# One product for two units: a windowed-attention pipeline's output projection, from float32 per unit to three float32r passes per pair

## The chip, the cores and the metric

The kernel runs on one core of a Trainium2 chip. The metric is device time in microseconds (us) of that core for one whole execution, as the median of several runs. The kernel before takes 2122.96 us (three runs, 2122.40 to 2123.63).

## The reference, cut to what matters

The program is a chain of layers over x of 8 x 512 tokens with 128 features. The change touches one kind of layer, used twice (`_L1_ffn_ref`, each time with two inner layers):

```python
def _layer(x, wqkv, qs, ksc, wo, lg, lb, w1, b1, w2, b2):
    h = shift_token(x)
    q, k, v = jnp.split(h @ wqkv, 3, axis=-1)          # 8 heads of 64: INNER = 512
    q, k = rotary_xpos(l2norm(q) * qs, l2norm(k) * ksc)
    o = local_attention(q, k, v)                        # windows of 64
    x = x + o @ wo                                      # 512 -> 128: the product of this case
    h = layer_norm(shift_token(x)) ; h = h @ w1 + b1
    a, g = jnp.split(h, 2, axis=-1)
    return x + (a * gelu(g)) @ w2 + b2
x = x + 0.5 * _L1_ffn_ref(layer_norm(x), ...)           # first of two uses
x = x + _L1_attn_ref(layer_norm(x), ...)
x = x + 0.5 * _L1_ffn_ref(layer_norm(x), ...)           # second
```

## The kernel before, in words

The program runs phases one after the other: two mixture-of-experts phases with a state-space phase between them, a setup of weights (`gated_setup_phase`), then `macaron_phase`, a short global phase, and `macaron_phase` again. Only the setup and the two macaron phases are touched.

A macaron phase treats 16 items (8 blocks of 512 tokens, for each of 2 inner layers), and each item is 4 units of 128 tokens. All engines run a software pipeline written out by hand: `item(i)` has one loop body for each t in 0 to 3, and that body is called **slot t** here. In a slot, the engines work on different units: with n the unit of the slot, TensorE makes the scores of n (`sims`), turns q and k of n+1 (`turn_qk`), makes attention times v of n-1 (`values`), projects q, k, v of n+3 (`project`), turns the probabilities of n (`turn_probs`, once for each of two halves r = 1 and r = 0), and makes the output product of n-1 (`output`). The parts of the gated feed-forward of an earlier item are spread over the slots: `up(.., 0, 2)` in slot 0, `centre` and `variance` in slot 1, `down` and three `up` in slot 2, two `up` in slot 3. In time order one item of the trace is slot 2, 3, 0, 1.

Each engine takes its instructions in the written order. Engines meet at semaphores. Those that matter here:

- `sims` (lines 1551, 1555, 1562) writes PSUM banks 2 and 3, which hold the turned probabilities of the unit before until ScalarE has copied them (`keep_turned`, line 1744). So `sims` waits for `pt_kept` of both halves.
- `turn_qk` (line 1533) writes banks 0 and 1, which VectorE reads in `rotate` (line 1830, two instructions a unit). It waits for `rotated`.
- `turn_probs` (line 1573) waits for `shared`: GpSimd multiplies the probabilities by the reciprocal sums (line 2058).
- `values` writes PSUM bank 4 (`O`), `keep_out` on VectorE (line 1881) copies it to `ot`, `output` (line 1600) multiplies by `wo` into the first 128 columns of O, and `add_out` (line 1889) adds that to the residual `u`.
- `f_take` on GpSimd (lines 1979, 1980), in slot 0, waits until all units of its item are added to `u`, and stands in GpSimd's queue ahead of `add(n + 3)` (line 2038) and so of the next slot's `share` (line 2058).

VectorE's order in a slot is `maxima` (1864), `keep_qt` (1857), `norms` (1841), `reciprocals` (1873), feed-forward pieces, `keep_out` (1881), `clip` (1849), `rotate` (1830), `add_out` (1889), `maxima` of the next unit (1864).

A float32 matmul stands in the trace as two rows, one for each of its passes over the array; a float32r matmul as one. `mm3` (lines 54 to 56) is a product in three float32r passes: high by high, low by high, high by low. Another phase, mixture of experts, has float32r matmuls of fewer columns, which the prediction reads:

```python
pe.matmul(bank[:, :2 * P], gh[:, q % 2, k, :], at(2 * P), start=k == 0, stop=False)      # line 384, 256 columns
mm = pe.matmul(bank[:, :P], gl[:, q % 2, k, :], at(P), start=False, stop=k == HC - 1)    # line 385, 128 columns
```

## Time and profile before

| | |
|---|---|
| median of 3 runs | 2122.96 us |
| profiled execution: its time, its span | 2117.76 us, 2115.9 us |
| TensorE matmul busy / weight loads busy | 1819.0 us (86%) / 1388.3 us (66%) |
| VectorE, ScalarE, GpSimd busy | 1571.3 us (74%), 1398.0 us (66%), 1284.5 us (61%) |
| mean granted TensorE clock | 0.937 of full speed |
| macaron phases, roughly | 660 to 1270 us and 1480 to 2100 us |

Busy time is the sum of an engine's rows. Matmul rows overlap, since each includes the way through the array, so a busy TensorE says only that its queue did not run dry; the pace is read from the starts of rows. PE is TensorE, PEld its weight loads, DVE VectorE, ACT ScalarE, POOL GpSimd.

### The profile page before, as it was taken

What the parts mean: (1) busy time and instruction counts of PE and PEld (TensorE: products, weight loads), DVE (VectorE), ACT (ScalarE), POOL (GpSimd) and SP (SyncE); (2) the same over time, 40 slices, a digit from 0 to 9 for tenths busy, and PEclk for the clock granted to TensorE, in tenths of its full rate; (3) what the DMA queues carried; (4) which work ended last, traced back from release to release, by engine and by line L of the source; (5) the groups of instructions that cost most, each with busy time, mean ns of one, the idle gap of its engine ahead of it and who ended that gap; (6) DMA issues with size and microseconds to landing.
All of it is one profiled execution on the core that took longest, in us unless ns stands there. A gap on an engine that the chain in (4) does not pass through costs nothing. (4 is left out here: it accounts for less than half of the span.)

```text
span 2115.9 us, 51807 instructions
## 1 busy us (share of the span) xinstructions
PE 1819.0 (86%) x16844; PEld 1388.3 (66%) x16845; DVE 1571.3 (74%) x2828; ACT 1398.0 (66%) x3956; POOL 1284.5 (61%) x1099
## 2 busy tenths in 40 slices
PE   4499776289955999999999997766999999999996
PEld 3488623278833777777777774334777777777773
DVE  6788767778855888788788883335888787888882
ACT  5555441345544888888878874555878888888783
POOL 3674300666415888878788872005888788787870
PEclk9999888589967999999999998788999999999998
DMA  6332310133151111111110110000110111111101
GB/s 210 86 91 57 84 54 1 56 97 87 39 149 44 27 29 22 25 24 27 24 28 21 22 29 1 4 0 18 27 29 20 27 24 27 24 26 22 25 22 40
DMA packets 87308, 88.26 MB, mean 42 GB/s; under 512 B 13978, under 2 KB 65863, under 8 KB 87016
## 3 DMA queue, kind: packets, MB, share of 16 engines
q1 hardware_dynamic: 77288, 68.09, 12.9%
q0 software_dynamic: 8704, 17.85, 2.5%
q8 instruction: 88, 1.44, 0.3%
q14 instruction: 76, 0.62, 0.1%
q10 hardware_dynamic: 1152, 0.25, 0.1%
HBM read 35.60 MB, written 22.22 MB: 27 GB/s over the span
## 5 line engine op out<-in xcount | busy, mean ns | idle before, releaser
L2058 POOL TENSOR_TENSOR mac_probs<-mac_probs,mac_prec 128x512 f32<-128x512 f32 x256 | 265.0, 1041 | 194.3 <-DVE mac_prec L1873 193.8
L1734 ACT ACTIVATE mac_probs<-banks,mac_nmax 128x128 f32<-128x128 f32 x1024 | 358.7, 385 | 0.0
L1830 DVE TENSOR_TENSOR route_pool<-banks,tables 128x1024 f32<-128x1024 f32 x256 | 300.6, 1214 | 33.7 <-ACT route_pool L1694 28.3
L2038 POOL TENSOR_TENSOR route_pool<-route_pool 128x1024 f32<-128x1024 f32 x128 | 303.3, 2369 | 35.7 <-issue 13.1
L1864 DVE TENSOR_REDUCE mac_nmax<-banks 128x4 f32<-128x512 f32 x256 | 164.8, 685 | 125.0 <-PE banks L1562 125.0
L2049 POOL TENSOR_TENSOR mac_qkn<-route_pool,mac_rc 128x1024 f32<-128x1024 f32 x128 | 243.6, 1903 | 16.4 <-issue 7.3
L876 POOL DMA_INDIRECT x_sorted<-route_pool,route_index x128 | 125.7, 982 | 185.8 <-DVE route_index L680 102.8
L1734 ACT ACTIVATION_READ_ACCUMULATOR mac_probs<-banks,mac_nmax 128x1 f32 x1024 | 231.9, 226 | 0.0
L884 POOL DMA_INDIRECT y_tokens<-moe_bench,moe_goal x144 | 140.7, 977 | 118.1 <-DVE moe_bench L827 77.9
L54 PE MATMUL banks<-wqkv_h,mac_hh 128*128 128x512 f32 x384 | 179.5, 467 | 27.0 <-POOL mac_hl L2013 22.1
L1744 ACT ACTIVATE mac_pts<-banks 128x512 f32<-128x512 f32 x256 | 147.2, 596 | 43.1 <-PE banks L1573 40.4
L1724 ACT ACTIVATE mac_kt<-banks 128x512 f32<-128x512 f32 x128 | 76.5, 597 | 139.6 <-PE banks L1533 139.3
L1694 ACT ACTIVATE route_pool<-banks 128x1024 f32<-128x1024 f32 x128 | 129.3, 1010 | 56.9 <-PE banks L56 56.8
L1573 PEld LDWEIGHTS banks<-ident,mac_probs 128*128 128x128 f32 x1024 | 118.9, 140 | 67.3 <-POOL mac_probs L2058 42.0
L1573 PE MATMUL banks<-ident,mac_probs 128*128 128x128 f32 x1024 | 150.1, 277 | 14.1 <-POOL mac_probs L2058 13.7
L56 PE MATMUL banks<-wqkv_l,mac_hh 128*128 128x512 f32 x384 | 155.0, 404 | 0.0
L384 PE MATMUL banks<-w,moe_gh 128*128 x576 | 152.1, 341 | 3.0 <-DVE moe_gl L817 2.8
L1841 DVE TENSOR_REDUCE mac_ss<-route_pool 128x16 f32<-128x1024 f32 x128 | 154.5, 1207 | 0.0
L555 ACT ACTIVATE moe_gh<-banks 128x512 fp32r<-128x512 f32 x144 | 86.1, 598 | 103.6 <-PE banks L373 102.9
L55 PE MATMUL banks<-wqkv_h,mac_hl 128*128 128x512 f32 x384 | 154.1, 401 | 0.0
L1533 PE MATMUL banks<-ident,mac_qkn 128*128 128x128 f32 x1024 | 141.6, 282 | 7.2 <-DVE route_pool L1830 7.2
L1600 PE MATMUL banks<-mac_ot,wo 128*128 128x128 f32 x1024 | 137.0, 277 | 5.0 <-DVE mac_ot L1881 5.0
(321 smaller groups left out, 5015.3 us busy)
## 6 DMA issues: line engine op xcount, KB each, us to landing
mac_v_even<-mac_v SPq DMA_DIRECT2D x224, 128.0 KB, 2.2
moe_xs<-x_sorted SPq DMA_DIRECT2D x144, 72.0 KB
route_pool<-y_tokens SPq DMA_DIRECT2D x16, 512.0 KB, 7.2
y_tokens<-moe_bench,moe_goal POOLq DMA_INDIRECT x144, 2.3
moe_bench<-in_L_attn_x SPq DMA_DIRECT2D x8, 256.0 KB, 6.0
route_pool<-in_L_ffn_W SPq DMA_DIRECT2D x4, 512.0 KB, 7.0
b<-in_b_flat SPq DMA_DIRECT2D x1, 2048.0 KB, 10.8
x_sorted<-route_pool,route_index POOLq DMA_INDIRECT x128, 2.3
```

Source lines behind the costliest of these rows:

```text
L54: pe.matmul(out, wh, xh, start=start, stop=False)
L55: pe.matmul(out, wl, xh, start=False, stop=False)
L56: return pe.matmul(out, wh, xl, start=False, stop=stop)
L384: pe.matmul(bank[:, :2 * P], gh[:, q % 2, k, :], at(2 * P), start=k == 0, stop=False)
L1573: tr = pe.transpose(m.ps[:, S + r, p * P:(p + 1) * P], probs[:, r, p, :], m.ident[:])
L1734: e = act.activation(probs[:, r, p, :], m.ps[:, S + r, p * P:(p + 1) * P], ACT.Exp, bias=nmax[:, r, p:p + 1], accum_out=psum[:, r, p:p + 1])
L1830: turn = dve.tensor_tensor(turned[:, i, :, :].rearrange("q k (h s j) -> q k h s j", s=2, j=DH // 2), q[:, :, :, ::-1, :] if i else q, tabl ...
L1841: dve.tensor_reduce(ss[:], squares[:].rearrange("q k (h d) -> q k h d", d=DH), AX.X, ALU.add).then_inc(ss_done, 1)
L1864: dve.tensor_reduce(nmax[:, r, :], m.ps[:, S + r, :].rearrange("q (p k) -> q p k", k=P), AX.X, ALU.max, negate=True).then_inc(maxed[r], 1)
L2038: pool.tensor_tensor(sums[:], turned[:, 0, :, :], turned[:, 1, :, :], ALU.add).then_inc(added, 1)
L2049: pool.tensor_tensor(qkn[:, t % 2, :, :].rearrange("q k (h d) -> q k h d", d=DH), sums[:].rearrange("q k (h d) -> q k h d", d=DH), rc[:].u ...
L2058: pool.tensor_tensor(probs[:, r, :, :], probs[:, r, :, :], prec[:, r, :].unsqueeze(2).to_broadcast([P, HP, P]), ALU.mult).then_inc(shared[ ...
```

## The change

The output product no longer runs once a unit in float32. It runs once for two units (a pair, 256 columns), in three float32r passes. For that VectorE makes from bank O an upper part `oh` (a copy rounded to float32r) and a lower part `ol` (bank O minus `oh`), each holding two units. `output` and `add_out` now stand only in slots 0 and 2, each for the pair that ended one slot before. The weights `wo` get an upper part (ScalarE) and a lower part (VectorE) in the setup phase. `fr` now shares the memory of `fq`, `fn` that of a third of `gate`, and three small constants live only as long as the phases that use them.

```diff
@@ -1309,7 +1309,7 @@
...
-        w.wo = sb(f"wo{l}", [P, HP, P])
+        w.woh, w.wol = sb(f"wo_h{l}", [P, HP, P], F32R), sb(f"wo_l{l}", [P, HP, P], F32R)
...
-                sp.dma_start(w.wo[:], ins["L1_ffn_wo"][l].rearrange("(j p) d -> p j d", p=P)).then_inc(rest_in, 16)
+                sp.dma_start(raw_wos[:, l, :, :], ins["L1_ffn_wo"][l].rearrange("(j p) d -> p j d", p=P)).then_inc(rest_in, 16)
...
@@ -1409,6 +1409,9 @@
             bias(0)
             bias(1)
             dve.tensor_scalar(raw1, raw1, lnw[:, 0, 0:1], None, ALU.mult).then_inc(steps[0], 1)
+            for l in range(2):
+                dve.wait_ge(wo_hi, START + l + 1)
+                dve.tensor_tensor(ws[l].wol[:], raw_wos[:, l, :, :], ws[l].woh[:], ALU.subtract)
             dve.wait_ge(steps[0], done + 2)
             split_weights(dve, [(raw1, w.w1h[:], w.w1l[:])], steps[0], done + 2)
 
+            act.wait_ge(rest_in, START + REST)
+            for l, w in enumerate(ws):
+                act.activation(w.woh[:].rearrange("p j d -> p (j d)"), raw_wos[:, l, :, :].rearrange("p j d -> p (j d)"),
+                               ACT.Copy).then_inc(wo_hi, 1)
 
...
-        pts, ot = sb("pts", [P, H2, T]), sb("ot", [P, HP, P])
-        fs, fq, fr, fn = sb("fs", [P, T]), sb("fq", [P, T]), sb("fr", [P, T]), sb("fn", [P, T])
+        pts = sb("pts", [P, H2, T])
+        oh, ol = sb("oh", [P, HP, H2 * P], F32R), sb("ol", [P, HP, H2 * P], F32R)
+        fs, fq = sb("fs", [P, T]), sb("fq", [P, T])
+        fr = fq
         fh, fl = sb("fh", [P, T], F32R), sb("fl", [P, T], F32R)
         gate = sb("gate", [P, MC, T])
+        fn = gate[:, 0, :]
         prod = spare[:, 8 * T:(8 + MC) * T].rearrange("q (i t) -> q i t", i=MC)
         zeroed, blanked = sem("zeroed"), sem("blanked")
         taken, hi_done, split = sem("taken"), sem("hi_done"), sem("split")
...
@@ -1579,7 +1590,10 @@
                     return
                 pe.wait_ge(v_kept, START + k + 1)
                 pe.wait_ge(v_copied[t], START + V_MOVES[t] * (j + 1))
-                pe.wait_ge(u_done, START + k)
+                if t % 2:
+                    pe.wait_ge(ol_kept, START + k)
+                else:
+                    pe.wait_ge(u_done, START + 2 * j + t // 2)
                 for r in range(H2):
                     pe.wait_ge(pt_kept[r], START + k + 1)
...
-            def output(k, j, lay):
-
-                if not live(k):
-                    return
-                wo = ws[layer(j, lay)].wo
-                pe.wait_ge(ot_kept, START + k + 1)
+            def output(j, s, lay):
+
+                if not there(j):
+                    return
+                w = ws[layer(j, lay)]
+                pe.wait_ge(ol_kept, START + NT * j + 2 * (s + 1))
                 for p in range(HP):
-                    mm = pe.matmul(m.ps[:, O, :P], wo[:, p, :], ot[:, p, :], start=(p == 0), stop=(p == HP - 1))
+                    mm = mm3(pe, m.ps[:, O, :H2 * P], (w.woh[:, p, :], w.wol[:, p, :]), (oh[:, p, :], ol[:, p, :]),
+                             start=(p == 0), stop=(p == HP - 1))
                 mm.then_inc(y_done, 1)
 
@@ -1665,7 +1680,8 @@
                     if t == 3:
                         up(i - 1, lay, 0, 1, G, gelued, MC * (i - 1) + 2)
                     turn_probs(n, 0)
-                    output(n - 1, before[0], lay)
+                    if t % 2 == 0:
+                        output(before[0], before[1] // 2, lay)
                     if t == 2:
                         up(i - 1, lay, 1, 0, F, f_normed, i)
@@ -1872,21 +1888,26 @@
                 dve.wait_ge(shared[r], START + k)
                 dve.reciprocal(prec[:, r, :], psum[:, r, :]).then_inc(recip[r], 1)
 
-            def keep_out(k):
+            def keep_out(k, j, t):
 
                 if not live(k):
                     return
                 dve.wait_ge(pv_done, PV_BASE + k + 1)
-                dve.wait_ge(y_done, START + k)
-                dve.tensor_copy(ot[:].rearrange("q p k -> q (p k)"), m.ps[:, O, :]).then_inc(ot_kept, 1)
-
-            def add_out(k, j, t, lay):
-
-                if not live(k):
-                    return
-                cols = bass.ds(start_of(j, lay) + t * P, P)
-                dve.wait_ge(y_done, START + k + 1)
-                dve.tensor_tensor(m.u[:, cols], m.ps[:, O, :P], m.u[:, cols], ALU.add).then_inc(u_done, 1)
+                if t % 2 == 0:
+                    dve.wait_ge(y_done, START + 2 * j + t // 2)
+                half = slice(t % 2 * P, (t % 2 + 1) * P)
+                dve.tensor_copy(oh[:, :, half], m.ps[:, O, :].rearrange("q (p k) -> q p k", k=P)).then_inc(oh_kept, 1)
+                dve.wait_ge(oh_kept, START + k + 1)
+                dve.tensor_tensor(ol[:, :, half], m.ps[:, O, :].rearrange("q (p k) -> q p k", k=P), oh[:, :, half],
+                                  ALU.subtract).then_inc(ol_kept, 1)
+
+            def add_out(j, s, lay):
+
+                if not there(j):
+                    return
+                cols = bass.ds(start_of(j, lay) + s * H2 * P, H2 * P)
+                dve.wait_ge(y_done, START + 2 * j + s + 1)
+                dve.tensor_tensor(m.u[:, cols], m.ps[:, O, :H2 * P], m.u[:, cols], ALU.add).then_inc(u_done, 1)
 
             def f_upper(j):
@@ -1952,10 +1973,11 @@
                     if t == 2:
                         f_upper(i - 1)
                         f_add(i - 2, lay)
-                    keep_out(n - 1)
+                    keep_out(n - 1, *before)
                     clip(n + 2)
                     rotate(n + 3, *ahead, lay)
-                    add_out(n - 1, *before, lay)
+                    if t % 2 == 0:
+                        add_out(before[0], before[1] // 2, lay)
                     maxima(n + 1, 1)
 
             dve.memset(v_even[:P // 2, 0, :, :], 0.0).then_inc(zeroed, 1)
@@ -2024,7 +2046,7 @@
 
                 if not there(j):
                     return
-                pool.wait_ge(u_done, START + NT * (j + 1))
+                pool.wait_ge(u_done, START + 2 * (j + 1))
                 pool.wait_ge(f_centred, START + j)
                 shifted(fs, f_taken, j, lay)
...
@@ -2310,15 +2332,16 @@
...
-        m.low_bf, m.ones_bf = sb("low_bf", [P, P], BF16), sb("ones_bf", [P, P], BF16)
-        m.blank, m.ids = sb("blank", [P, WIDE]), sb("ids", [P, PAIRS // P + 1])
+        m.ids = sb("ids", [P, PAIRS // P + 1])
+            m.low_bf, m.ones_bf = [moe.enter_context(nc.sbuf_tensor(n, [P, P], BF16)) for n in ("low_bf", "ones_bf")]
+            m.blank = moe.enter_context(nc.sbuf_tensor("blank", [P, WIDE], F32))
```

**TensorE, end of slot 0.** The order around the product in the loop over items, before:

```order
L55 MATMUL banks<-wqkv_h,mac_hl 128x512
L56 MATMUL banks<-wqkv_l,mac_hh 128x512
L1573 MATMUL banks<-ident,mac_probs 128x128 x8
L1600 MATMUL banks<-mac_ot,wo 128x128 x4
L1551 MATMUL banks<-masks_bf,both_bf 64x512 x4
L1562 MATMUL banks<-mac_kt,mac_qt 64x128 x16
```

and now, the last nine of the twelve passes and what follows (`sims`, lines 1562 and 1573 now):

```order
L54 MATMUL banks<-mac_oh,wo_h 128x256
L55 MATMUL banks<-mac_oh,wo_l 128x256
L56 MATMUL banks<-mac_ol,wo_h 128x256
L54 MATMUL banks<-mac_oh,wo_h 128x256
L55 MATMUL banks<-mac_oh,wo_l 128x256
L56 MATMUL banks<-mac_ol,wo_h 128x256
L54 MATMUL banks<-mac_oh,wo_h 128x256
L55 MATMUL banks<-mac_oh,wo_l 128x256
L56 MATMUL banks<-mac_ol,wo_h 128x256
L1562 MATMUL banks<-masks_bf,both_bf 64x512 x4
L1573 MATMUL banks<-mac_kt,mac_qt 64x128 x16
```

Four float32 matmuls (eight passes) became twelve passes of 256 columns in the same place.

**TensorE, end of slot 1**, before:

```order
L56 MATMUL banks<-wqkv_l,mac_hh 128x512
L1573 MATMUL banks<-ident,mac_probs 128x128 x4
L1617 ISA
L1618 MATMUL banks<-mac_fq,mean_of 128x512
L1573 MATMUL banks<-ident,mac_probs 128x128 x4
L1600 MATMUL banks<-mac_ot,wo 128x128 x4
L1551 MATMUL banks<-masks_bf,both_bf 64x512 x4
```

and now:

```order
L56 MATMUL banks<-wqkv_l,mac_hh 128x512
L1584 MATMUL banks<-ident,mac_probs 128x128 x4
L1632 ISA
L1633 MATMUL banks<-mac_fq,mean_of 128x512
L1584 MATMUL banks<-ident,mac_probs 128x128 x4
L1562 MATMUL banks<-masks_bf,both_bf 64x512 x4
L1573 MATMUL banks<-mac_kt,mac_qt 64x128 x16
```

Nothing stands any more between the last turned probabilities (line 1584) and the next unit's `sims` (line 1562). Slot 3 is the same.

**VectorE, slot 3**, before:

```order
L1873 RECIPROCAL mac_prec<-mac_psum 128x4
L1915 SCALAR_TENSOR_TENSOR route_pool<-banks,w_bias,mac_gate 114x512
L1873 RECIPROCAL mac_prec<-mac_psum 128x4
L1881 COPY mac_ot<-banks 128x512
L1849 TENSOR_SCALAR mac_rc<-mac_rn 128x16
L1830 TENSOR_TENSOR route_pool<-banks,tables 128x1024 x2
L1889 TENSOR_TENSOR u<-banks,u 128x128
```

and now:

```order
L1889 RECIPROCAL mac_prec<-mac_psum 128x4
L1936 SCALAR_TENSOR_TENSOR route_pool<-banks,w_bias,mac_gate 114x512
L1889 RECIPROCAL mac_prec<-mac_psum 128x4
L1899 CAST mac_oh<-banks 128x4x128
L1901 TENSOR_TENSOR mac_ol<-banks,mac_oh 128x4x128
L1865 TENSOR_SCALAR mac_rc<-mac_rn 128x16
L1846 TENSOR_TENSOR route_pool<-banks,tables 128x1024 x2
L1880 TENSOR_REDUCE mac_nmax<-banks 128x4
```

One instruction more stands ahead of `clip` and `rotate` in every slot; the add is gone from slots 1 and 3.

## Rows read from the trace of the kernel before

**Rows 1.** Busy time by stage: span; PE, PEld, DVE, ACT, POOL; clock; DMA

```profile
675.00:1260.00 585.00, 577.37 (x6533) 448.42 (x6532) 486.69 (x755) 473.72 (x1511) 470.34 (x374) 1.00 0.11 25
```

**Rows 2.** Waits, 800 to 1200 us: waiting, releaser, total us, times, longest

```profile
DVE mac_nmax L1864 <- PE banks L1562: 42.0, 42, 2.7
```

**Rows 3.** TensorE's timeline, masks that open a slot: start us, us, what

```profile
1001.06 0.41 PE L1551 MATMUL banks<-masks_bf,both_bf 64*64 64x512 bf16 x4
...
1022.31 0.41 PE L1551 MATMUL banks<-masks_bf,both_bf 64*64 64x512 bf16 x4
...
1030.68 0.41 PE L1551 MATMUL banks<-masks_bf,both_bf 64*64 64x512 bf16 x4
...
1039.78 0.41 PE L1551 MATMUL banks<-masks_bf,both_bf 64*64 64x512 bf16 x4
```

**Rows 4.** Timeline, weight loads of the output product and of what follows it

```profile
1009.91 0.97 PEld L1600 LDWEIGHTS banks<-mac_ot,wo 128*128 128x128 f32 x8
...
1010.80 0.18 PEld L54 LDWEIGHTS banks<-mac_fh,w_h 128*114 128x114 f32 x1
...
1029.59 0.97 PEld L1600 LDWEIGHTS banks<-mac_ot,wo 128*128 128x128 f32 x8
```

**Rows 5.** TensorE's timeline in the first mixture phase: float32r, 256 and 128 columns

```profile
131.06 0.33 PE L384 MATMUL banks<-w,moe_gh 128*128 x1
131.23 0.22 PE L385 MATMUL banks<-w,moe_gl 128*128 x1
131.29 0.33 PE L384 MATMUL banks<-w,moe_gh 128*128 x1
```

**Rows 6.** TensorE's timeline, slot 2, second and third `up` after the product

```profile
1012.07 0.40 PE L56 MATMUL banks<-mac_fl,w_h 128*114 128x512 f32 x1
1012.71 0.46 PE L54 MATMUL banks<-mac_fh,w_h 128*113 128x512 f32 x1 [0.24 <-ACT mac_v L1715]
```

**Rows 7.** Timeline, copies of turned probabilities, next weight load of `sims`

```profile
1021.52 0.60 ACT L1744 ACTIVATE mac_pts<-banks 128x512 f32<-128x512 f32 x1 [0.53 <-PE banks L1573]
...
1068.50 1.09 ACT L1744 ACTIVATE mac_pts<-banks 128x512 f32<-128x512 f32 x2 [0.45 <-PE banks L1573]
...
1069.65 0.14 PEld L1551 LDWEIGHTS banks<-masks_bf,both_bf 64*64 64x64 bf16 x4 [0.30 <-issue]
```

**Rows 8.** VectorE's timeline in the global phase: upper part, lower part, next instruction

```profile
1402.97 0.42 DVE L2217 CAST glob_xh<-glob_ln_xn 128x512 fp32r<-128x512 f32 x1
1403.42 0.69 DVE L2219 TENSOR_TENSOR glob_xl<-glob_ln_xn,glob_xh 128x512 fp32r<-128x512 f32 x1
1404.03 0.68 DVE L2242 SCALAR_TENSOR_TENSOR glob_qn<-glob_rn,banks 128x512 f32<-128x512 f32 x1
```

**Rows 9.** Timeline, end of slot 3 and `turn_qk` of slot 0

```profile
1019.34 0.66 DVE L1881 COPY mac_ot<-banks 128x512 f32<-128x512 f32 x1
...
1019.92 0.75 DVE L1849 TENSOR_SCALAR mac_rc<-mac_rn 128x16 f32<-128x16 f32 x1
...
1020.58 2.34 DVE L1830 TENSOR_TENSOR route_pool<-banks,tables 128x1024 f32<-128x1024 f32 x2
...
1023.73 1.09 PE L1533 MATMUL banks<-ident,mac_qkn 128*128 128x128 f32 x8
```

**Rows 10.** Timeline, from the add of slot 0 to GpSimd's shares of slot 1

```profile
1031.57 0.28 DVE L1889 TENSOR_TENSOR u<-banks,u 128x128 f32<-128x128 f32 x1
...
1032.10 0.60 POOL L1979 COPY mac_fs<-u 64x512 f32<-64x512 f32 x1 [0.40 <-DVE u L1889]
...
1033.45 2.38 POOL L2038 TENSOR_TENSOR route_pool<-route_pool 128x1024 f32<-128x1024 f32 x1
...
1035.78 2.05 POOL L2058 TENSOR_TENSOR mac_probs<-mac_probs,mac_prec 128x512 f32<-128x512 f32 x2
```

**Rows 11.** Timeline, the last work of the setup phase on VectorE and GpSimd

```profile
651.61 0.87 DVE L109 TENSOR_TENSOR w_l<-last_raw_gated_w,w_h 128x682 fp32r<-128x682 f32 x1
...
653.30 1.39 POOL L109 TENSOR_TENSOR w_l<-last_raw_gated_w,w_h 128x682 fp32r<-128x682 f32 x1
```

More of the change, by code:

```diff
@@ L1328, in gated_setup_phase @@
         raws, raw1s = sb("raw_qkv", [P, 2, 3 * T]), sb("raw_gated_w1", [P, 2, 2 * HID])
-        raw_masks = sb("raw_masks", [P, 2, T])
+        raw_masks, raw_wos = sb("raw_masks", [P, 2, T]), sb("raw_wo", [P, 2, HP, P])
         scales, lnw, b1 = sb("qk_scales", [P, 2, 4, DH]), sb("ln_w", [P, 2, 2]), sb("b1_raw", [P, 2, 2 * MC])
@@ L1332, in gated_setup_phase @@
         rest_in, rest2_in, extras_in = sem("rest_in"), sem("rest2_in"), sem("extras_in")
-        biased, steps, cleared = sem("biased"), [sem(f"steps{l}") for l in range(2)], sem("cleared")
+        biased, steps, cleared, wo_hi = sem("biased"), [sem(f"steps{l}") for l in range(2)], sem("cleared"), sem("wo_hi")
         block = c.block()
@@ L1487, in macaron_phase @@
         pt_done, pt_kept = [sem(f"pt_done{r}") for r in range(H2)], [sem(f"pt_kept{r}") for r in range(H2)]
-        pv_done, ot_kept, y_done, u_done, v_kept = sem("pv_done"), sem("ot_kept"), sem("y_done"), sem("u_done"), sem("v_kept")
+        pv_done, oh_kept, ol_kept, y_done, u_done, v_kept = (
+            sem("pv_done"), sem("oh_kept"), sem("ol_kept"), sem("y_done"), sem("u_done"), sem("v_kept"))
         v_copied = [sem(f"v_copied{t}") for t in range(NT)]
```

## The prediction

> **What bounds the kernel now.** I read the busy time by stage first. In the first macaron phase TensorE's matmul rows fill 577 of 585 us [rows 1], VectorE's 487, ScalarE's 474, GpSimd's 470: TensorE's queue hardly runs dry, and each of the others has about a fifth of its time free. The waits say the same: in 400 us VectorE waits 42.0 us for TensorE's scores, once in each of 42 units [rows 2]. So TensorE paces the pipeline, and by its starts I measure. The masks that open a slot give the lengths [rows 3]: slot 0 is 1030.68 - 1022.31 = 8.37 us, slot 1 is 9.10, slots 2 and 3 together 21.25, an item 38.72. There are 32 items (16 in each of two phases).
>
> But matmul rows include the way through the array and lie over each other, so small waits do not show as idle. I therefore looked at what stands beside the output product. While it runs, ScalarE copies the turned probabilities that the next `sims` will overwrite: 1021.52 to 1022.12, and the masks start at 1022.31, only 0.19 us later [rows 3, 7]. In a tighter place the next weight load starts 1069.65 - 1069.59 = 0.06 us after such a copy ends [rows 7], so 0.06 is what the semaphore takes, and 0.13 is the whole slack. The output product is the cover of that copy.
>
> **TensorE's pass.** Before, the first weight load of the product is at 1029.59 and `sims` starts at 1030.68: 1.09 us for eight passes [rows 3, 4]. Where `up` follows it is 1010.80 - 1009.91 = 0.89, so 0.11 a pass, and about 0.20 for the change to the small tiles of `sims` [rows 4]. Passes of 256 float32r columns do not occur in these phases. The nearest rows are in the mixture phase: a 256-column and a 128-column pass together take 131.29 - 131.06 = 0.23 us, of which 0.17 and 0.06 by the starts of the matmuls [rows 5]. The bounds for one pass are 0.06 and 0.23 (the pair's whole time). I take half the pair, 0.115, since both passes of it bring their own 128-column weights like those here. Twelve passes are 1.38 us: +0.49 over the 0.89 of eight. Counting passes alone, a pair saves 2 x 0.89 - 1.38 = 0.40 us.
>
> **VectorE's part.** `keep_out` to `clip` is 1019.92 - 1019.34 = 0.58 us now [rows 9]. The upper and lower parts stand in the global phase: the cast ends at 1403.39, the subtraction starts 0.03 later, and the next instruction 0.61 after that [rows 8]. The copy from PSUM stays at 0.66, so copy and subtraction take 0.66 + 0.03 + 0.61 = 1.30: +0.72 us ahead of `clip` and `rotate` in every slot. The subtraction would have to be free or hidden to cost less; nothing in the rows lets it exceed its own 0.69 and a semaphore, so 0.6 to 0.8 are the bounds. The add of 256 columns is an estimate between 128 columns in 0.28 [rows 10] and 1024 in half of 2.34 [rows 9]: 0.41, so +0.13 in slots 0 and 2 and -0.28 in slots 1 and 3.
>
> **One item, slot by slot** (shift of the slot's end against before):
>
> Slot 2. The product is 0.49 longer. Behind it the third `up` waits for ScalarE's copy of v: it starts at 1012.71, and would start at 1012.07 + 0.23 = 1012.30 [rows 6]. That takes 0.41 of it. VectorE's +0.72 goes into its waits, which are longest here. Left: +0.07.
>
> Slot 3. No product. TensorE goes from the turned probabilities straight to `sims` and waits for the copy: the load can start at 1022.12 + 0.06 = 1022.18 instead of 1022.31 [rows 3, 7]. Of the 1.09 us removed, 0.13 comes back; the rest is a new wait. Shift of the end: 0.07 - 0.12 = -0.05. VectorE's `rotate` ends at 1022.92 before, now 0.07 + 0.72 later, at 1023.71.
>
> Slot 0. `turn_qk` waits for that `rotate`: 1023.71 + 0.06 against 1023.73 before [rows 9], so +0.07 (GpSimd's `norm`, behind the later `clip`, ends at about the same time). Then the long product with nothing behind it but `sims`: +0.49, less 0.03 that the probabilities' multiplication gave in waiting before. Shift at the end: +0.53.
>
> Slot 1. VectorE's add in slot 0 ended at 1031.85 [rows 10]. Now the second part (+0.72, beside the +0.07) and the wider add (+0.13) stand before it: 1032.77, +0.92. GpSimd's `f_take` waits for it, and its queue is full from there: copies, 2.38 us of `add`, and the shares begin at 1035.78, 0.05 before the end of the `add` [rows 10]. So the shares come 0.92 to 0.94 later, while TensorE arrives only about 0.6 later: it waits for GpSimd, and turns the probabilities 0.94 late. No product follows, which gives back 0.12: +0.82 at the end.
>
> Slots 1 and 2 meet there, and slot 2 absorbs VectorE's remaining lag (after its `rotate` nothing needs it until the three `up`, nine passes of 0.23 us [rows 6], and the next `sims` are through). So the shift does not grow within the next item: **+0.82 us an item**, 38.72 to 39.54. 32 x 0.82 = +26 us. Fill and drain of the two phases follow the same slots and are in the 32.
>
> Setup: two subtractions of 0.69 us more on VectorE, ahead of its last split, which ends at 651.61 + 0.87 = 652.48; GpSimd's split ends at 654.69 [rows 11]. 652.5 + 1.4 = 653.9 is still inside: 0. ScalarE's two casts wait for nothing late. If the cover were gone it would be 1.4 us once. The shared memories add no wait: `fn` is written after the last use of `gate`'s third, and `up` waits for its reader before the next. The moved constants cost nothing in time.
>
> The profiled execution took 2117.76 us, so this sum gives 2144; the median of the runs is 5.2 us above it, which gives **2149 us**.
>
> One page is to be weighed here. The stage row shows weight loads busy 448 of 585 us, 77%, and VectorE 83% [rows 1]. The Trainium skill, "Perfetto Trace Analysis", section "Identifying the Most-Contended Engine", says that matmul busy time misleads, that TensorE is judged by its weight loads' share, and that the engine with the highest share is the one to optimize. By it VectorE would be the bound and not TensorE; what that gives is the fourth case below. The wait of VectorE for scores in every unit [rows 2] speaks against it.
>
> **The rivals.**
>
> 1. TensorE's passes are the bound and the copy of the probabilities does not take the product's place. Then an item saves two pairs' 0.40 us, 0.8 us, and with the 0.41 us of slot 2's wait up to 1.2: 26 to 39 us less, 2084 to 2097. For it: TensorE's rows leave nothing idle [rows 1]. Against: the copy ends 0.19 us before `sims` now, and it cannot start before the probabilities are turned [rows 7].
>
> 2. TensorE's terms as above, but GpSimd's and VectorE's lateness in slots 0 and 1 stays hidden. Then the item is 0.07 - 0.12 + 0.49 - 0.12 = +0.32 us, up to +0.5 with half of the rest: +10 to +16 us, 2133 to 2139. For it: VectorE still waits 1.0 us a unit for scores. Against: the shares of slot 1 start without any idle time after the `add` [rows 10].
>
> 3. The twelve passes cost 0.23 us each, the upper bound: 1.4 us more for each pair, 2.8 an item, about 90 us beyond the forecast, 2239. It would need 256 columns to be no faster than 512.
>
> 4. VectorE is the bound: every unit gets 0.72 longer, less 0.07 for the adds: 128 x 0.65 = +83 us, 2206. It decides once VectorE's waits are used up; they are 1.0 us a unit for scores and some tenths more for others, so +0.65 leaves it just short of it.
>
> **How the numbers follow.** The forecast has 0.60, rival 1 0.13, rival 2 0.16, rival 3 0.02, rival 4 0.05, and 0.04 for no change through terms that cancel. The terms that are least sure are GpSimd's in slot 1 (0.29) and the two products (0.49 each): a tenth of a microsecond in each of four slots is 13 us. The forecast's own range is 2138 to 2165. The range takes in rival 2 and a stronger VectorE term: 2126 to 2170; rival 1 and the tails of 3 and 4 stay out. A measurement of this kernel tells 0.2%, 4 us, from no change. Faster 0.14 (rival 1 and a little of rival 2), same 0.05, slower 0.81.
>
> **What would show it.** In the new profile: the twelve passes from first load to `sims` in slot 0 take 1.58 us; in slots 1 and 3 `sims` starts about 0.06 us after the second copy of turned probabilities, with TensorE or its loads idle some 0.8 us before it, put down to ScalarE's copy; VectorE's wait for scores falls from 1.0 us a unit to under 0.5; TensorE's wait for GpSimd's shares in slot 1 grows by about 0.3 us an item. An item is 39.5 us, slot 0 longer by 0.6, slots 3 shorter by 0.1. The prediction is wrong if `sims` in slots 1 and 3 starts at once after the turned probabilities, if an item is shorter than 38.7, or if the passes are not at 0.115.

## The result and the profile after

The changed kernel takes **2149.59 us** (median of 4 runs, 2148.54 to 2150.79), beside 2122.68 us for the kernel before in the same comparison: a ratio of 1.0127, with a 95% interval of 1.0109 to 1.0144. The forecast was 2149, range 2126 to 2170. The total is right. Of its terms the cover and the price of a pass are right; what it gave slot 2 and slot 1 is wrong, and these errors nearly cancel, which is the larger part of what follows.

The page of the kernel after begins with its span and the engines' busy time:

```profile
span 2147.9 us, 51298 instructions
PE 1798.6 (84%) x16588; PEld 1368.2 (64%) x16589; DVE 1618.1 (75%) x2894; ACT 1402.7 (65%) x3958; POOL 1287.2 (60%) x1099
```

The stretches of the first macaron phase, answering to [rows 1], with the same columns:

```profile
675.00:1275.00 600.00, 566.69 (x6420) 439.09 (x6420) 508.40 (x788) 477.47 (x1517) 474.99 (x378) 1.00 0.11 25
```

The window is 600 us here, 585 there, since the phase is longer. TensorE's matmul rows fell from 577 of 585 to 567 of 600 and its weight loads from 448 to 439: the product is smaller, as meant. TensorE now has 33 us in which no matmul row runs, against 8. VectorE went from 487 to 508. The work that TensorE lost came back as waiting.

The waits of 800 to 1200 us say for whom (engine, line and tile, what released it: us in total, times, longest), answering to [rows 2]:

```profile
DVE mac_nmax L1880 <- PE banks L1573: 40.4, 30, 2.6
PEld banks L1562 <- issue: 23.6, 30, 1.2
POOL mac_fs L2001 <- DVE u L1910: 8.9, 11, 0.9
PE banks L1562 <- issue: 8.8, 12, 0.7
PE banks L1562 <- ACT mac_pts L1760: 6.9, 8, 1.0
PE banks L54 <- DVE mac_ol L1901: 2.0, 3, 0.7
```

Line 1562 is the masks, the first matmul of `sims`. Before, only their weight loads waited, for 4.1 us in 11 places. Now the matmuls wait too, 12 times put down to nothing that the profile shows ("issue") and 8 times to ScalarE's copy. The last row is the other new wait, of the product for the lower part.

### The slots

I took the start of the masks' first weight load in every slot, and of each kind of slot in the first phase the median length (us). A length by the masks' matmuls can differ by 0.03. The items of inner layer 0 and of inner layer 1 differ, which the forecast did not look for:

| kernel | slot 2 | slot 3 | slot 0 | slot 1 | item |
|---|---|---|---|---|---|
| before, layer 0 | 12.45 | 8.78 | 8.37 | 9.10 | 38.71 |
| after, layer 0 | 12.61 | 8.64 | 8.93 | 8.97 | 39.14 |
| before, layer 1 | 12.45 | 8.79 | 8.40 | 9.19 | 38.82 |
| after, layer 1 | 13.54 | 8.79 | 8.93 | 9.01 | 40.27 |

From the first `sims` to the last of each phase, both phases together took 1211.6 us before and 1241.7 after: **+30.1 us**. Start, global phase and end account for +2 us. So little outside the macaron phases moved, and an average item is 0.94 us longer, where 0.82 was forecast: 0.43 in layer 0, 1.45 in layer 1 (1.58 in the second phase, where slot 3 of layer 1 is 0.12 longer). The profiled executions differ by 31.9 us (2117.76 and 2149.66) and the medians by 26.9, as the profiled one of before was a quick one; the +26 of the sum stands against the 31.9.

**Slot 3 and slot 1: the copy takes the product's place.** ScalarE, TensorE's loads and TensorE at the end of slot 3, answering to [rows 7] (start, length, engine, line, what; idle time before it):

```profile
1026.96 0.60 ACT L1760 ACTIVATE mac_pts<-banks 128x512 f32<-128x512 f32 x1 [0.53 <-PE banks L1584]
1027.63 0.14 PEld L1562 LDWEIGHTS banks<-masks_bf,both_bf 64*64 64x64 bf16 x4 [0.94 <-issue]
1027.66 0.41 PE L1562 MATMUL banks<-masks_bf,both_bf 64*64 64x512 bf16 x4 [0.73 <-issue]
```

The copy ends at 1027.56, the masks' load starts 0.07 later, and TensorE had been idle for 0.73 us. "Issue" says that the profile names no releaser. The copy's end is what fits: the load follows it by 0.07 in every slot 1 of both phases, and so it does in this item's slot 3. The slot is 0.14 shorter, for 1.09 us of passes removed.

Not every slot 3 is like this one. Items 2 to 5 and 10 to 13 of a phase run in a loop, the others are written out one by one. Where slot 3 leads into an item of the loop, the masks' load starts 0.21 us after the copy:

```profile
830.97 0.60 ACT L1760 ACTIVATE mac_pts<-banks 128x512 f32<-128x512 f32 x1 [0.45 <-PE banks L1584]
831.77 0.14 PEld L1562 LDWEIGHTS banks<-masks_bf,both_bf 64*64 64x64 bf16 x4 [1.08 <-issue]
```

It was 0.21 in these places before as well, where the forecast's place had 0.19. So there was no slack to return, and these slots 3 have the same length before and after (8.78 in layer 0, 8.79 in layer 1). The 8.64 of the table stands for the written-out items of layer 0, and the 0.00 of layer 1 is the loop's. That the loop costs the 0.14 us is an inference from where it occurs; no run takes an item out of the loop.

**Slot 0: the passes.** TensorE's loads of the product, first and last, and the masks behind it:

```profile
1034.93 0.19 PEld L54 LDWEIGHTS banks<-mac_oh,wo_h 128*128 128x128 f32 x1
...
1036.23 0.19 PEld L56 LDWEIGHTS banks<-mac_ol,wo_h 128*128 128x128 f32 x1
...
1036.55 0.41 PE L1562 MATMUL banks<-masks_bf,both_bf 64*64 64x512 bf16 x4
```

Eleven passes from 1034.93 to 1036.23 are 0.118 each, and the whole 1.62 us, against 1.09 [rows 3, 4].

**Slot 2 in layer 1: a wait that was not forecast.** VectorE and TensorE there, after:

```profile
1131.37 0.74 DVE L1947 SCALAR_TENSOR_TENSOR u<-banks,b,u 128x512 f32 x1
1132.24 1.51 DVE L1951 SCALAR_TENSOR_TENSOR x<-u,x  x1
1133.68 0.68 DVE L1899 CAST mac_oh<-banks 128x512 fp32r<-128x512 f32 x1
1134.39 0.69 DVE L1901 TENSOR_TENSOR mac_ol<-banks,mac_oh 128x512 fp32r<-128x512 f32 x1
...
1133.41 1.03 PE L1584 MATMUL banks<-ident,mac_probs 128*128 128x128 f32 x8
1135.13 0.38 PE L54 MATMUL banks<-mac_oh,wo_h 128*128 128x256 f32 x1 [0.69 <-DVE mac_ol L1901]
```

And the same place before:

```profile
1124.50 1.50 DVE L1930 SCALAR_TENSOR_TENSOR x<-u,x  x1
1125.92 0.68 DVE L1881 COPY mac_ot<-banks 128x512 f32<-128x512 f32 x1
1126.65 1.16 PE L1600 MATMUL banks<-mac_ot,wo 128*128 128x128 f32 x8
```

In the second inner layer VectorE closes the item of two before with an update of `x`, 1.5 us, and this stands ahead of `keep_out`. Before, the copy was through at 1126.60 and the product started 0.05 later. It had waited a little for it even then (the waits of before, 800 to 1200 us):

```profile
PEld banks L1600 <- DVE mac_ot L1881: 0.6, 3, 0.2
```

Three times 0.2 us, once in each item of layer 1 in that stretch: there was no slack at all. Now the lower part is ready only at 1135.08, and TensorE stands idle for 0.69 us before the product. In layer 0 there is no such update.

**The clip.** The one group of VectorE that got shorter without being edited, of the whole kernel, before and after (out<-in, shape, count | busy us, mean ns of one | idle before):

```profile
L1849 DVE TENSOR_SCALAR mac_rc<-mac_rn 128x16 f32<-128x16 f32 x128 | 87.1, 680 | 9.8 <-ACT mac_rn L1704 9.8
```

```profile
L1865 DVE TENSOR_SCALAR mac_rc<-mac_rn 128x16 f32<-128x16 f32 x128 | 53.9, 421 | 3.6 <-ACT mac_rn L1720 3.6
```

So of the forecast's +0.65 us of VectorE a unit 0.26 was taken back here on average. It is not even: in slot 3 the clip fell from 0.72 to 0.75 us to 0.17, in slot 0 it stayed near 0.6.

### The profile page after: what moved, and what is told of

It reads as the page before. It is cut to its first block and busy times, and to the rows that moved or that the text cites. A ratio compares the mean times of both kernels' runs of the same rounds, so it can differ in the third digit from the quotient of the medians.

```text
span 2147.9 us, 51298 instructions
## 1 busy us (share of the span) xinstructions
PE 1798.6 (84%) x16588; PEld 1368.2 (64%) x16589; DVE 1618.1 (75%) x2894; ACT 1402.7 (65%) x3958; POOL 1287.2 (60%) x1099
## 3 DMA queue, kind: packets, MB, share of 16 engines
q0 software_dynamic: 8704, 17.85, 2.4%
## 5 line engine op out<-in xcount | busy, mean ns | idle before, releaser
L54 PE MATMUL banks<-wqkv_h,mac_hh 128*128 128x512 f32 x384 | 178.7, 465 | 26.9 <-POOL mac_hl L2035 22.0
L1573 PE MATMUL banks<-mac_kt,mac_qt 64*64 64x128 f32 x4096 | 140.8, 270 | 0.0
```

The costliest lines, as they stand in the source:

```text
L54: pe.matmul(out, wh, xh, start=start, stop=False)
```

## The experiments

Twelve kernels ran, in three groups, on chips where everything ahead of the macaron phases takes some 60 to 70 us longer (the kernel before is at 2180 to 2188 there), while the slots have the lengths that they have above, to 0.03 us. So each ratio is to the kernel before on the same chip, and the working goes by slots. "Slots" are slot 2, 3, 0, 1 of layer 0, then of layer 1, in the first phase. "By slots" is the difference of the items, times 8 items for each layer and phase, 32 in all; for the changed kernel it is +31 us to before. Executions of one kernel spread by some 5 us there to either side, and what the slots and what the medians give differ by up to 10 us as well. The changed kernel itself was not repeated there, but the run named "another clip" below, whose slots are the changed kernel's, is 27.8 us above before.

### Where the product covers the copy

**The kernel before, without the product in slots 3 and 1:**

```diff
                 pe.wait_ge(ot_kept, START + k + 1)
+                if skip:                       # odd slots
+                    pe.sem_inc(y_done, 1)
+                    return
```

> The kernel before, with the output product left out in slots 1 and 3 (the add there takes whatever bank O holds); slots 0 and 2 keep their float32 product. Theory A (the product is only the cover of ScalarE's copy of the turned probabilities): sims starts 0.06 us after that copy instead of 0.19, so slots 1 and 3 get 0.12 us shorter each, an item 0.25, the kernel 8 us: about 2115 us (2108 to 2118). Rival (TensorE's passes are the bound): 0.89 to 1.09 us less in each of the two slots, 32 items: 57 to 70 us less, 2053 to 2066.

Ratio 0.9962 (0.9948 to 0.9976). Slots 12.47, 8.67, 8.40, 8.98 and 12.47, 8.79, 8.41, 9.08; 3.7 us less by slots. 64 products of 1.09 us are gone, 70 us of TensorE's work, and the medians differ by 7.9. That ends rival 1: in these two slots the product was cover. Layer 1's slot 3 gave nothing back, as it did in the changed kernel.

**The changed kernel with the probabilities turned ahead of `variance` and of the first `up`,** so that these stand where the product stood:

```diff
+                    turn_probs(n, 0)
                     if t == 1:
                         variance(i - 1)
                     if t == 3:
                         up(i - 1, lay, 0, 1, G, gelued, MC * (i - 1) + 2)
-                    turn_probs(n, 0)
```

> The changed kernel with variance (slot 1) and the second up (slot 3) moved from between the two halves of turned probabilities to behind them, so that they stand beside ScalarE's last copy. Theory A (slots 1 and 3 end with TensorE waiting for that copy): slot 3 falls by about 0.2 us (then GpSimd's share, turning, copy are the chain), slot 1 by 0.3 us: 0.5 an item, 16 us less than the changed kernel, ratio to before 1.005 (1.003 to 1.007). Rival (no such wait, or the later half of the probabilities is no sooner there): nothing, ratio 1.0127.

Ratio 1.0099 (1.0080 to 1.0118). Slot 1 went from 8.97 to 8.72 and in layer 1 from 9.01 to 8.81, slot 3 only from 8.64 to 8.61. By slots that is 8 us less than after; the medians give some 4 (22.6 above before). The theory holds in slot 1. In slot 3 the median hides two cases: in the written-out items 6 to 8 it fell from 8.63 to 8.47, in items 3 and 4, of the loop, it stayed at 8.78 to 8.80. The last load of the probabilities now starts 0.33 us after GpSimd's last share ends, in both cases. That share ends at 7.06 in the first and at 7.20 in the second (us from the slot's start), and without the move the load stood at 7.55 in both. So in slot 3 TensorE now runs up to the shares, which are the next thing that it waits for.

### VectorE's part by itself

**The kernel before with the subtraction added** (it writes a tile that nobody reads, and the product waits for it; passes and their order unchanged; to make room, `fr` and `fn` share memory as in the changed kernel):

```diff
                 [copy of the attention output].then_inc(ot_kept, 1)
+                dve.wait_ge(ot_kept, START + 2 * k + 1)
+                dve.tensor_tensor(ol[:].rearrange("q p k -> q (p k)"), m.ps[:, O, :],
+                                  ot[:].rearrange("q p k -> q (p k)"), ALU.subtract).then_inc(ot_kept, 1)
...
-                pe.wait_ge(ot_kept, START + k + 1)
+                pe.wait_ge(ot_kept, START + 2 * k + 2)
```

> The kernel before with VectorE's part alone: after the copy of bank O a subtraction of the same size, whose result nobody reads but for which the product waits; one float32 product and one add a unit as before. Theory A (VectorE's 0.72 us goes into a shorter clip and into waits, except behind the x update): items of inner layer 0 grow by at most 0.4 us (turn_qk of slot 1 has only 0.2 us to spare), items of inner layer 1 by 0.7 to 1.2 us, most of it in slot 2, where the x update delays the subtraction: 14 to 26 us more, 2137 to 2149. Theory B (as in the prediction, GpSimd's lateness in slot 1 in every item): 0.3 to 0.5 us in slot 1 of both layers alike, none in slot 2: 10 to 16 us more, and equal items in both layers.

Ratio 1.0083 (1.0060 to 1.0105). Slots 12.45, 8.76, 8.37, **9.48** and **12.98**, 8.79, 8.39, 9.52; 20 us more than before by slots, 18.4 by medians. The whole of it lies in slot 1 (+0.38 and +0.33) and, in layer 1, in slot 2 (+0.53). Slots 3 and 0 did not move by more than 0.02. Had VectorE been the bound, 0.69 in each of 128 units would be 88. TensorE and GpSimd in slot 1 of this kernel:

```profile
986.86 1.09 PE L1536 MATMUL banks<-ident,mac_qkn 128*128 128x128 f32 x8 [0.21 <-DVE route_pool L1833]
987.25 0.60 POOL L1985 COPY mac_fs<-u 64x512 f32<-64x512 f32 x1 [0.73 <-DVE u L1895]
990.95 2.04 POOL L2064 TENSOR_TENSOR mac_probs<-mac_probs,mac_prec 128x512 f32<-128x512 f32 x2
992.05 0.43 PEld L1576 LDWEIGHTS banks<-ident,mac_probs 128*128 128x128 f32 x4 [0.31 <-POOL mac_probs L2064]
```

This is the chain of the forecast's slot 1: the add is late, GpSimd's `f_take` waits for it, its queue carries the lateness to the shares, and TensorE waits for the shares. It gives 0.38, not 0.7, since `rotate` ahead of the add is later by less than the subtraction is long (see below).

**The changed kernel without the subtraction** (the lower part is zero throughout):

```diff
-                dve.wait_ge(oh_kept, START + k + 1)
-                dve.tensor_tensor(ol[:, :, half], [attention output], oh[:, :, half],
-                                  ALU.subtract).then_inc(ol_kept, 1)
```

> The changed kernel without the subtraction: the lower part stays zero, so the products lose the lower part of the attention output; all twelve passes run. Theory A: items of layer 0 stay at 39.1 us (within 0.1), slot 2 of layer 1 loses TensorE's wait of 0.7 us for the lower part, up to 0.8 us: 11 to 14 us less, 2136 to 2139. Theory B (VectorE's part costs in slot 1 of every item): 0.3 to 0.4 us less in slot 1 of both layers, 10 to 13 us less as well, but alike in both layers. Which slots give it back tells them apart.

Ratio 1.0058 (1.0035 to 1.0081). Slots 12.61, 8.71, 8.94, 8.97 and **12.84**, 8.82, 8.93, 8.97; 11 us less than after by slots (12.4 above before by medians, so some 15 less). Layer 0 hardly changed (slot 3 by 0.07 in the first phase, not in the second): with the longer product in place, the subtraction costs nothing there. It costs 0.70 in slot 2 of layer 1. The clip was back at a mean of 596 ns, which took back a quarter of the 0.69 us that the subtraction left.

### The update of x

**The changed kernel with the update behind the add of slot 2:**

```diff
-                if l == 1:                     # in f_add, ahead of keep_out
-                    dve.wait_ge(f_added, START + j + 1)
-                    dve.scalar_tensor_tensor(out=m.x[:, cols], in0=m.u[:, cols], scalar=0.5, in1=m.x[:, cols], ...
...
                         add_out(before[0], before[1] // 2, lay)
+                    if t == 2:
+                        x_add(i - 2, lay)
```

> The changed kernel with the x update of inner layer 1 (1.5 us on VectorE in slot 2) moved from ahead of the upper and lower parts to behind the add of u. Theory A: slot 2 of layer 1 falls from 13.54 to about 12.6 us, 16 items: 15 us less, about 2134 (2131 to 2138); layer 0 unchanged. Theory B: VectorE's sum in the slot is the same, so nothing changes: 2149.

Ratio 1.0084 (1.0061 to 1.0106). Slot 2 of layer 1 is **12.60**, as in layer 0, and the other slots are those of after: 15 us less by slots. The medians show less, 17.5 us above before and so some 10 less than the changed kernel. VectorE and TensorE in that slot:

```profile
1195.98 0.68 DVE L1899 CAST mac_oh<-banks 128x512 fp32r<-128x512 f32 x1
1196.69 0.69 DVE L1901 TENSOR_TENSOR mac_ol<-banks,mac_oh 128x512 fp32r<-128x512 f32 x1
...
1200.53 0.88 DVE L1956 SCALAR_TENSOR_TENSOR x<-u,x  x1
```

```profile
1198.15 0.36 PE L54 MATMUL banks<-mac_oh,wo_h 128*128 128x256 f32 x1
```

The parts are ready 0.77 us ahead of the product, which waits for nothing, and the update itself takes 0.88 us instead of 1.51 in its new place (2.77 in two of the 16). Half of the 31 us of the slots is this one order.

**Both moves together:**

> The changed kernel with both moves: variance and the second up behind the turned probabilities, and the x update behind the add of u. Theory A: the two gains add, 16 us and 17 us (what the phases gave in the run with the x update alone), ratio to before 0.997 (0.995 to 1.000), the first version below the kernel before. Rival (they overlap, one hides the other): not under 1.003.

Ratio 1.0027 (1.0013 to 1.0040). Slots 12.58, 8.61, 8.92, 8.75 and 12.56, 8.78, 8.93, 8.80. By slots the two add up: 8 and 15 alone, 23 together, and the medians agree (5.6 above before, some 22 less than the changed kernel). It is not below the kernel before.

### The product's length

**One pass of three** (upper part of the weights with upper part of the output alone; the other two products are left out, the two parts are still made):

```diff
-                    mm = mm3(pe, m.ps[:, O, :H2 * P], (w.woh[:, p, :], w.wol[:, p, :]), (oh[:, p, :], ol[:, p, :]),
-                             start=(p == 0), stop=(p == HP - 1))
+                    mm = pe.matmul(m.ps[:, O, :H2 * P], w.woh[:, p, :], oh[:, p, :], start=(p == 0), stop=(p == HP - 1))
```

> The changed kernel with only the high-by-high pass of the product: 4 passes of 256 columns instead of 12, so the product is not exact. Theory A (the copy of the turned probabilities is a floor under every slot end): the 0.94 us of passes come back in part only. Slot 0 falls from 8.92 to 8.25 to 8.3 us (product with the change to small tiles 0.66 us, then the floor), slot 2 of layer 0 from 12.6 to 12.4 (the third up waits for the copy of v again), slot 2 of layer 1 from 13.5 to 12.6; slots 1 and 3 stay. Item -0.8 us in layer 0, -1.5 in layer 1: 37 us less than the changed kernel, ratio to before 0.995 to 0.997. Rival (passes bind in full): 0.94 us in slots 0 and 2 of all 32 items, 60 us less, ratio 0.984.

Ratio 1.0050 (1.0034 to 1.0067), a miss. Slots 12.49, 8.65, **8.28, 9.59** and 12.59, 8.79, 8.32, 9.64. Slots 0 and 2 came as expected, slot 1 not: slot 0 gave back most of its eight passes (-0.65), and slot 1 took that again (+0.62). TensorE and GpSimd in slot 1:

```profile
985.45 1.09 PE L1544 MATMUL banks<-ident,mac_qkn 128*128 128x128 f32 x8 [0.30 <-DVE route_pool L1845]
985.98 0.60 POOL L2000 COPY mac_fs<-u 64x512 f32<-64x512 f32 x1 [0.86 <-DVE u L1909]
990.77 0.42 PEld L1584 LDWEIGHTS banks<-ident,mac_probs 128*128 128x128 f32 x4 [0.44 <-POOL mac_probs L2079]
```

**A float32 product of 256 columns** (no parts and no subtraction, in the setup neither; one matmul for each quarter, which stands as two rows in the trace):

> The pair's product in float32 (eight passes of 256 columns), VectorE with the copy alone, otherwise the changed kernel: pairing without the split. By the starts of the 512-column float32 rows (about 0.43 us a pass) a pass is 0.215 us, a product 1.72. Theory A: slot 0 is 8.92 + 1.72 - 1.41 = 9.2 us, slot 2 of layer 0 12.9, slot 2 of layer 1 about 13.1 (no wait for the lower part but a longer product), slots 1 and 3 as in the changed kernel: item 39.8 in both layers, ratio to before 1.015 to 1.018. Rival (VectorE's part and not the place of the product made the change slower): slots 0 and 2 as before but for the passes, ratio under 1.008.

Ratio 1.0121 (1.0104 to 1.0139). Slots 12.92, 8.64, **9.24**, 8.97 and 13.14, 8.79, 9.24, 8.97. Slots 0 and 2 of layer 0 each grew by 0.31 over the changed kernel's. Slot 2 of layer 1 is shorter by 0.40, without the subtraction. The slots came as expected, the ratio not: by slots this kernel is some 38 us above before, by medians 27.8. In its profiled execution everything outside the two phases took 967 us, against 974 to 982 in the three other versions of its group, so the difference lies outside the phases; what makes it is not shown. For TensorE the three float32r passes are the quicker of the two.

### The order of reciprocals, and the clip

**Both moves, and in slot 3 the reciprocals ahead of VectorE's feed-forward product:**

```diff
+                    reciprocals(n, 0)
                     if t == 3:
                         product(i - 1, lay, 0)
-                    reciprocals(n, 0)
```

> The version with variance, the second up and the x update moved (e6), and in slot 3 the reciprocal of the later half ahead of VectorE's feed-forward product instead of behind it. Theory A (with the cover in place, slot 3 ends by the chain reciprocal, share, turning, copy): the reciprocal starts 0.45 us sooner, slot 3 falls from 8.61 to 8.1 to 8.2 us, 32 items: 13 to 16 us less than e6, ratio to before 0.996 (0.994 to 0.998), faster than the kernel before. Rival (slot 3 is bound by TensorE's passes or by rotate): nothing, ratio 1.0027.

Ratio 1.0059 (1.0043 to 1.0074), a miss. Slot 3 fell to 8.34 (-0.27), as it should if the shares were late there: the last share ends 0.31 sooner in the items of the loop, and ScalarE's copy ends 0.31 sooner. But slot 0 rose to 9.35 (+0.43). VectorE's product now delays the two parts, the clip and `rotate`, for which the next slot's `turn_qk` waits. `rotate` starts 7.86 us into slot 3, against 7.31 without this move.

**The same three moves in the kernel before:**

> The kernel before, float32 product in every slot, with the same three moves (variance and second up behind the turned probabilities, x update behind the add, reciprocal first in slot 3). Theory A (before, the product covers the copy and TensorE's passes set every slot): no gain, ratio 0.998 to 1.001. Rival (the moves help whatever the product): as much as on the changed kernel, some 45 us, ratio 0.98.

Ratio 1.0092 (1.0077 to 1.0107), worse, not equal: slots 12.45, 9.13, 8.37, 9.56 in layer 0, 18.9 us above before by medians. Where the product still stands between the probabilities and `sims`, taking `variance` and `up` away from in front of them leaves TensorE waiting for the shares: 14.0 us in 400, against 6.1 in the kernel before. How much each of the three moves did was not separated.

**The changed kernel with another clip** (a reduction over an axis of one in place of tensor_scalar; the limit of 1e12 is left out):

```diff
-                dve.tensor_scalar(rc[:], rn[:], 1e12, None, ALU.min).then_inc(clipped, 1)
+                dve.tensor_reduce(rc[:], rn[:].unsqueeze(3), AX.X, ALU.max).then_inc(clipped, 1)
```

> The changed kernel with that clip alone, limit left out. Theory A: clip under 0.25 us in all 128 units; items of layer 0 stay at 39.1 us and of layer 1 at 40.3 (the product in slot 2 waits for the lower part, which stands before the clip). Rival: clip unchanged.

It ran once. All the clips of the whole kernel:

```profile
L1865 DVE TENSOR_REDUCE mac_rc<-mac_rn 128x16 f32<-128x16 f32 x128 | 20.3, 159 | 3.6 <-ACT mac_rn L1720 3.6
```

and no slot changed by more than 0.03: 12.61, 8.64, 8.93, 8.97 and 13.54, 8.82, 8.92, 8.98. So what VectorE saves there is not on the path of the changed kernel.

**The reciprocals' kernel with that clip:**

> e12 with the clip made by a tensor_reduce over one element in place of tensor_scalar with min; it leaves out the limit at 1e12. Theory A (the clip's 0.5 to 1.3 us is waiting for the GpSimd instruction that runs beside it, a matter of the tensor_scalar form): every clip takes under 0.25 us, VectorE gets some 0.3 us a slot free. The time moves little, since rotate has room in slots 2, 3 and 0: 0 to 8 us less than e12. Rival (the clip is slow because its input is late or because GpSimd slows any instruction): the clip stays at 0.4 to 0.7 us on the mean.

Ratio 1.0020 (1.0010 to 1.0029), the best of the versions that keep the pairs. Slots 12.67, 8.35, 9.35, **8.29** and 12.64, 8.46, 9.37, 8.39: slot 1 is 0.46 shorter than in the kernel without it. That is what the reciprocals' move had cost in slot 0: slots 0 and 1 together are 17.64 here, 18.10 without the clip and 17.67 with the two moves alone. By slots it is level with before (item 38.67 and 38.86). In its profiled execution the global phase was 3 us longer and the end 5 than in that of before. No version that keeps the pairs beat the kernel before. The first two moves with the new clip, without the reciprocals', was not run.

## Why the prediction was right, and where not

**The cover was right, where there was slack.** In the written-out items of layer 0, where the forecast was read, slot 3 is 0.14 shorter and slot 1 is 0.13 (0.12 forecast), the load is 0.07 us behind the copy, the idle time 0.73 (some 0.8). Taking the product away alone gave 0.11 and 0.12. In the slots 3 that lead into the loop there was nothing to give back, and the forecast's -0.12 is 0.00. Rival 1 is excluded.

**The price of a pass was right.** 0.118 measured, 0.115 taken from the pair; the product is +0.53, the forecast +0.49. Slot 0 became +0.56 for +0.58.

**The step that failed first: "VectorE's +0.72 goes into its waits, which are longest here".** This was slot 2, +0.07. It is +0.16 in layer 0 and +1.09 in layer 1. The forecast was read from items of layer 0, where VectorE comes to `keep_out` early. In layer 1 the update of `x` stands ahead of it, and VectorE was just in time: the copy ended at 1126.60, the product started at 1126.65. There the lag goes into TensorE's wait. Moving the update gave back 15 of 31 us by slots. Its row was in the trace of before, and so was the wait of 0.2 us: the items of the second layer had to be read by themselves.

**The step that failed second: slot 1 at +0.29, by a lag of VectorE in slot 0 of 0.92.** Slot 1 is -0.13, the missing product's cover and nothing else. The forecast set the two delays side by side, as is right: the shares' 0.92 to 0.94 against TensorE's own 0.6, and the longer one counts. It is the size of the first that was wrong. Counted from the opening of slot 0 in the item of [rows 3], VectorE's add ends 0.63 later (9.54 to 10.17 us). The forecast's 0.92 was 0.07 for the slot's own shift, 0.72 for the second part and 0.13 for the wider add. The add's 0.13 came. The other 0.50 is `rotate`, in place of 0.72. Before, `rotate` stood there behind two things:

```profile
1028.26 1.00 ACT L1694 ACTIVATE route_pool<-banks 128x1024 f32<-128x1024 f32 x1
...
1028.54 0.64 DVE L1849 TENSOR_SCALAR mac_rc<-mac_rn 128x16 f32<-128x16 f32 x1
1029.30 2.35 DVE L1830 TENSOR_TENSOR route_pool<-banks,tables 128x1024 f32<-128x1024 f32 x2
```

The clip ended at 1029.18, but `rotate` also waits for ScalarE's squares of q and k (line 1694), which ended at 1029.26. Now the clip, 0.61 long, is the later of the two, and `rotate` follows it at once:

```profile
1034.60 0.61 DVE L1865 TENSOR_SCALAR mac_rc<-mac_rn 128x16 f32<-128x16 f32 x1
1035.12 2.34 DVE L1846 TENSOR_TENSOR route_pool<-banks,tables 128x1024 f32<-128x1024 f32 x2
```

So 0.2 us of the 0.72 went into a gap that the forecast had not read. In slot 3 the lag of `rotate` is smaller still, 0.13 to 0.16 us, and there the reason is the clip, which fell to 0.17. GpSimd's shares of slot 1 begin 0.64 later, and TensorE's first load of these probabilities 0.63 later (14.57 to 15.20). Without the subtraction that load stands at 15.09, though the shares begin at 13.65 there instead of 14.11: TensorE's own path is 0.52 longer. The 0.11 between them is gone at the end of the slot. TensorE's wait for the shares, which was to grow, is 6.1 us in 400 before and 6.5 after. The chain itself exists: with the subtraction alone slot 1 takes +0.38. Slots 0 and 1 together (layer 0) show it:

| kernel | slot 0 | slot 1 | sum |
|---|---|---|---|
| before | 8.37 | 9.10 | 17.47 |
| before with the subtraction | 8.37 | 9.48 | 17.85 |
| one pass of three | 8.28 | 9.59 | 17.87 |
| after | 8.93 | 8.97 | 17.90 |
| after without the subtraction | 8.94 | 8.97 | 17.91 |

Either cause alone makes the sum 17.85 to 17.91, both together the same. The first two kernels still have a product at the end of slot 1, the other three have none; so the table shows that the causes do not add, and not by how little each misses the other.

So the +0.82 of an item was made of slots +0.07, -0.12, +0.58, +0.29, and measured in layer 0 as +0.16, -0.14, +0.56, -0.13 (+0.43), in layer 1 as +1.09, 0.00, +0.53, -0.18 (+1.45). Layer 0 alone is rival 2's case (+0.32 to 0.5), which had a chance of 0.16. That the total agreed is luck: slot 2 is some 18 us above the forecast over the 32 items, slot 1 some 14 below it. The agreement to 1 us is luck once more. The forecast added 5.2 us for the distance of the profiled execution of before from its median, and the changed kernel's profiled execution lies at its median. Profile to profile it is +31.9 for +26.

**Rival 4 and the page behind it.** VectorE's wait for scores did not fall to 0.5 us a unit: it is 40.4 us in 400, in 30 waits, against 42.0 in 42 [rows 2]. VectorE is the busiest by the share of busy time, 508 of 600 us, and the Trainium skill's "Perfetto Trace Analysis" (section "Identifying the Most-Contended Engine") would name it. Adding 0.7 us to each of its 128 units cost 18 to 20 us, a fifth of the whole. The trace does not agree with that rule here: VectorE is not full, and what decides is which wait ends last at the end of each slot.

**What stays open.** Why slots and medians differ by up to 10 us in some versions. Whether the moves cost something outside the phases: in the profiled executions of the four versions of the changed kernel with the first move the global phase is 3 to 4 us longer and the end 3 to 5; with another clip and no move the global phase was 2 us longer as well, and executions there spread by as much.

## What to carry to other kernels

When a pass is taken off an in-order engine, look at what the next instruction waits for besides that engine: if another engine's copy ends with the pass, the pass was cover, and shortening it returns only the slack (here nothing to 0.18 us of 1.09). Two delays on parallel chains count by the longer one where they meet, so each must be sized by itself, with every wait on its way: an instruction that already waits for a second thing takes up part of a delay (here 0.2 of 0.72 us). And where the items of a loop differ, read the slack of each kind: an update that runs in one of two layers made 15 of 31 us.

## What the runs showed of the hardware

**A small VectorE instruction beside a large one of GpSimd.** The clip, 16 columns, takes 0.17 us where no GpSimd tensor_tensor runs. In the kernel before that is so in 2 of 128; in the other 126 the median is 0.70 us and the longest 1.27, and nearly all of these end some 0.03 us after GpSimd's instruction does, whenever they began. In the changed kernel the two parts move the clip, 46 run alone, and the mean falls from 680 to 421 ns. Two clips of the changed kernel, of slot 3 and of slot 0:

```profile
1026.08 0.17 DVE L1865 TENSOR_SCALAR mac_rc<-mac_rn 128x16 f32<-128x16 f32 x1
...
1034.60 0.61 DVE L1865 TENSOR_SCALAR mac_rc<-mac_rn 128x16 f32<-128x16 f32 x1
```

As a tensor_reduce over the same 16 columns it is 159 ns in all 128, of which 82 begin beside a tensor_tensor of GpSimd. The Trainium skill's "SBUF — State Buffer", section "Who interferes with whom", says that a tensor_scalar can take the port pair that VectorE shares with GpSimd, that the pair is locked for a whole instruction, and that a tensor_reduce never takes it. The trace agrees, with 704 ns against 159. The same section says that a VectorE instruction with two inputs in the SBUF contends with a GpSimd one that reads it; the update of `x` is of that kind, 1.51 us in front and 0.88 where it was moved, and no run here shows which of GpSimd's instructions it waits for.

**A wait in the loop.** In the changed kernel TensorE's weight load of the masks starts 0.07 us after the copy that it waits for where the next item is written out, and 0.21 us after it (once 0.36) where the next item is one of the loop.

**Passes of 256 columns.** A float32r pass with new weights takes 0.118 us, where one of 512 columns takes 0.23 [rows 6]: halving the columns halves the time here, and the weights' reload shows nowhere.
